# A two-block decoder on one core: layer norms in two parts of two row tiles

## What is computed

```
x = ln(x + causal attention(x))                 # 32 heads, 8 key heads, rope, scaled keys
x = ln(x + fake_quant(x) @ fake_quant(ctx))     # per sequence, 512x512
x = ln(x + stream mixing(x))                    # 24 logits a row, 50 Sinkhorn rounds on 4x4, branch
x = ln(x + gated decay attention(x))            # 32 heads, chunks of 128
x = ln(x + cross attention(x, ctx))             # 32 heads, keys and values of ctx, rms norms
x = ln(x + x @ W.T + bias + low-rank product)   # rank 16 x 3, selected by sequence
```

## Time and profile before

| | us |
|---|---|
| median of 3 runs | 1503.37 |
| lowest and highest | 1503.25, 1508.79 |
| the profiled execution | 1506.34 |
| its span | 1504.5 |
| TensorE busy | 1433.5 (95%) |
| VectorE busy | 1051.2 (70%) |
| ScalarE busy | 808.9 (54%) |
| POOL busy | 582.5 (39%) |

### The profile page before, as it was taken

The page is one execution under the profiler, slowest core; times in us unless marked ns, Lnnn a source line. Parts: engine busy times, 40 slices in busy tenths (PEclk is TensorE's granted clock), DMA queues, the critical chain, the costliest instruction groups (busy, mean ns, idle before and its releaser), DMA issues.

```text
span 1504.5 us, 23551 instructions
## 1 busy us (share of the span) xinstructions
PE 1433.5 (95%) x7346; PEld 1181.5 (79%) x7346; DVE 1051.2 (70%) x2415; ACT 808.9 (54%) x2066; POOL 582.5 (39%) x611
## 2 busy tenths in 40 slices
PE   7999999998999989999999999789999999999976
PEld 5888888886688868778778877578888888888862
DVE  5697666795587876776776687557667676676662
ACT  4556655554223255755765675346656656565440
POOL 4555444433022145655755663323223123132010
PEclk9999999999899999999999999889999999999998
DMA  8011111012023241222133130410201201201000
GB/s 314 1 71 71 71 70 65 10 67 115 0 85 126 85 141 51 104 98 99 56 107 116 33 122 29 182 42 1 84 15 71 85 15 70 76 22 62 1 1 28
DMA packets 30126, 107.66 MB, mean 72 GB/s; under 512 B 3847, under 2 KB 13191, under 8 KB 22104
## 3 DMA queue, kind: packets, MB, share of 16 engines
q1 hardware_dynamic: 30040, 106.58, 19.7%
HBM read 97.07 MB, written 9.50 MB: 71 GB/s over the span
## 4 chain that ended last, share of the span: by engine, by line
PE 64%; issue 13%; DVE 11%; POOL 8%; ACT 3%; DMA 1%; POOLq 0%; SPq 0%; DVEq 0%; ACTq 0%
PE bank L186 11%; PE bank L187 11%; PE bank L188 11%; PE bank L1743 7%; PE bank L1571 6%; PE bank L1729 3%; POOL yss L1377 2%; PE bank L316 2%; PE bank L1687 2%; PE bank L339 1%; POOL wq_low L1018 1%; POOL tmp L159 1%; PE bank L1201 1%; PE bank L285 1%; PE bank L327 1%
## 5 line engine op out<-in xcount | busy, mean ns | idle before, releaser
L159 POOL TENSOR_TENSOR tmp<-tmp,sin 128x512 f32<-128x512 f32 x80 | 111.8, 1397 | 210.9 <-ACT tmp L152 210.9
L2003 DVE SCALAR_TENSOR_TENSOR logit<-bank,qss,amask 128x512 f32<-128x512 f32 x128 | 91.5, 749 | 86.3 <-PE bank L188 85.0
L188 PE MATMUL bank<-wo_low,att_high 128*128 128x512 f32 x384 | 150.7, 393 | 0.0
L1743 PE MATMUL bank<-probT,v 128*128 128x256 f32 x512 | 123.6, 384 | 1.2 <-ACT probT L1849 1.2
L1925 POOL TENSOR_TENSOR qss<-qss,half 128x4 f32<-128x4 f32 x32 | 34.8, 1089 | 229.2 <-DVE qss L1989 229.2
L1849 ACT ACTIVATE probT<-bank 128x512 f32<-128x512 f32 x128 | 69.6, 595 | 86.0 <-PE bank L1729 85.9
L1571 PE MATMUL bank<-kT,wg 128*128 128x256 f32 x512 | 112.9, 383 | 2.9 <-ACT prob L1605 2.9
L1840 ACT ACTIVATE prob<-logit,rmax 128x512 f32<-128x512 f32 x128 | 91.5, 716 | 39.1 <-DVE rmax L2007 39.1
L1571 PEld LDWEIGHTS bank<-kT,wg 128*128 128x128 f32 x512 | 98.1, 192 | 17.2 <-ACT prob L1605 3.3
L186 PE MATMUL bank<-l_wo_high,att_high 128*128 128x512 f32 x256 | 104.9, 410 | 1.8 <-DVE att_low L1461 1.1
L1743 PEld LDWEIGHTS bank<-probT,v 128*128 128x128 f32 x512 | 94.0, 190 | 13.9 <-issue 1.8
(11 more groups left out here) (262 smaller groups left out, 4100.2 us busy)
## 6 DMA issues: line engine op xcount, KB each, us to landing
wq<-in_l_wq SPq DMA_DIRECT2D x16, 1024.0 KB, 5.9
wo<-in_l_wo SPq DMA_DIRECT2D x16, 1024.0 KB, 4.9
wkv<-in_l_wkv SPq DMA_DIRECT2D x16, 512.0 KB, 5.8
wg<-in_l_wg SPq DMA_DIRECT2D x8, 1024.0 KB, 4.8
wq<-in_x_wq SPq DMA_DIRECT2D x8, 1024.0 KB, 7.2
wo<-in_x_wo SPq DMA_DIRECT2D x8, 1024.0 KB, 4.9
kT<-in_x_wkv SPq DMA_DIRECT2D x8, 512.0 KB, 4.2
kv_keys<-logit SPq DMA_DIRECT2D x8, 512.0 KB, 4.7
```

The costliest lines, as they stand in the source:

```text
L159: eng.tensor_tensor(halves(tmp[4 + j % 2]), halves(tmp[2 + j % 2]), per_batch(sin), ALU.mult).then_inc(sem(f"{l}_sinp"), 1)
L188: return eng.matmul(dst, a_high, b_low, start=False, stop=stop)
L1743: last = pe.matmul(bank[VALUE_BANKS[s % 2]][:, 0:L], v[at][:, b * CT + kt, :], probT[s % 2][:, kt, :], start=(kt == 0), stop=(kt == CT - 1))
L2003: dve.scalar_tensor_tensor(logit[s % 2][:, c, :], bank[3 + c][:, :], qss[p][:, 1, h, 2 * b + c:2 * b + c + 1], amask[:, c, :], ALU.mult, A ...
```

## The change

Every norm is cut in two parts, k = 0 with tiles 0 and 1, k = 1 with tiles 2 and 3 (`PAIRS`): `ln_stats`, `ln_spread`, `ln_rows` on VectorE, and `ln_gpsimd`, `ln_tensor`, `ln_scalar`, `ln_split` with an argument k. The power is on two columns. In the three attentions tiles 0 and 1 are added earlier, and their part of the norm stands ahead of the adds of tiles 2 and 3. In the second sublayer the product of tile 0 stands ahead of the first norm's second turns. The second norm's turns stand on both sides of the early unit, and ScalarE squares and copies by parts. In the third norm the rows of tiles 0 and 1 stand ahead of the last statistic. In the last sublayer the low-rank product is done by sequence, in two banks, and the turns of tiles 2 and 3 stand after the four products of tile 0. The selection moves to step 5 of the cross attention's last group, the high query weights to step 5 of the first attention's last group, and POOL's first key power behind both parts of the fourth norm. The fourth norm's tiles are turned into other banks.

```diff
@@ l0_scalar, body
+                    if s == 5 and last:
+                        l1_high_queries(act)
...
                 if last:
                     turned(7)
                     headed(7)
-                    l1_high_queries(act)
@@ l0_vector, body
-                    if s == 7 and not last:
+                    if s == 7:
                         if first:
                             dve.wait_ge(sem("ld_x"), 16)
                         residual_add(dve, "l0", g, 0, bank[0])
...
                 if last:
                     rest(6)
+                    residual_add(dve, "l0", g, 1, bank[1])
+                    ln_stats(dve, 0, 0, "l0_added", 4 * g)
                     rest(7)
-                    homes = [bank[0], bank[1], bank[L0_LATE[0]], bank[L0_LATE[1]]]
-                    sums_and_stats(dve, 0, lambda t: residual_add(dve, "l0", g, t, homes[t]), "l0_added", 4 * g)
+                    ln_rows(dve, 0, 0)
+                    for t in PAIRS[1]:
+                        residual_add(dve, "l0", g, t, bank[L0_LATE[t - 2]])
+                    ln_stats(dve, 0, 1, "l0_added", 4 * g)
@@ the norm's helpers
+        PAIRS = ((0, 1), (2, 3))
+        def turn_bank(n, t):
+            return bank[([0, 1, 2, 5] if n == 3 else [6, 5, 7, 2])[t]]
+        def ln_stats(dve, n, k, done, before):
+            for t in PAIRS[k]:
+                dve.wait_ge(sem(done), before + t + 1)
+                dve.bn_stats(stat[:, t, :], x[:, t, :]).then_inc(sem("ln_stat"), 1)
+            ln_spread(dve, n, k)
+        def ln_spread(dve, n, k):
+            seen = 2 * NT * n + NT * k
+            for i, t in enumerate(PAIRS[k]):
+                dve.wait_ge(sem("ln_stat"), seen + i + 1)
                 dve.bn_aggr(mv[:, t, :], stat[:, t, :]).then_inc(sem("ln_stat"), 1)
+            dve.wait_ge(sem("ln_stat"), seen + NT)
+            dve.tensor_scalar(lnr[:, 0, 2 * k:2 * k + 2], mv[:, 2 * k:2 * k + 2, 1], LN_EPS, None, ALU.add)\
+               .then_inc(sem("ln_var"), 1)
+        def ln_rows(dve, n, k):
+            dve.wait_ge(sem("ln_rstd"), 2 * n + k + 1)
+            for t in PAIRS[k]:
                 dve.tensor_scalar(x[:, t, :], x[:, t, :], mv[:, t, 0:1], lnr[:, 1, t:t + 1],
                                   ALU.subtract, ALU.mult).then_inc(sem("ln_x"), 1)
@@ cross_vector
+            quantised(0)
+            ln_rows(dve, 0, 1)
+            quantised(1)
+            quantised(2)
+            add(0)
+            quantised(3)
+            add(1)
+            ln_stats(dve, 1, 0, "rows_added", 0)
+            ln_rows(dve, 1, 0)
+            add(2)
+            add(3)
+            ln_stats(dve, 1, 1, "rows_added", 0)
+            ln_rows(dve, 1, 1)
@@ mix_scalar
+            for k in range(2):
+                for t in PAIRS[k]:
+                    act.wait_ge(sem("ln_x"), NT * 1 + t + 1)
+                    act.activation(tmp[t][:, :], x[:, t, :], ACT.Square, accum_out=ssq[:, 0, t:t + 1])\
+                       .then_inc(sem("mix_ssq"), 1)
+                ln_scalar(act, 1, k)
+                if k == 0:
+                    kv_copy(act, 1)
@@ mix_vector
                 if t:
                     stats(t - 1)
+                if t == 2:
+                    ln_spread(dve, 2, 0)
+            ln_rows(dve, 2, 0)
             stats(NT - 1)
+            ln_spread(dve, 2, 1)
+            ln_rows(dve, 2, 1)
@@ l1_vector, body
                 gated(3)
+                if last_group:
+                    for t in PAIRS[0]:
+                        residual_add(dve, "l1", g, t, bank[L1_OUT[t]])
                 rest(2)
                 rest(3)
                 if last_group:
+                    ln_stats(dve, 3, 0, "l1_added", 4 * g)
+                    ln_rows(dve, 3, 0)
+                    for t in PAIRS[1]:
+                        residual_add(dve, "l1", g, t, bank[L1_OUT[t]])
+                    ln_stats(dve, 3, 1, "l1_added", 4 * g)
@@ x_vector, body
-                    if s == 7 and not last_group:
+                    if s == 7:
                         add(g, 0)
...
+                    if s == 5 and last_group:
+                        ffn_select(dve)
...
                 if last_group:
                     low(6)
+                    add(g, 1)
+                    ln_stats(dve, 4, 0, "x_added", 4 * g)
                     low(7)
+                    ln_rows(dve, 4, 0)
+                    for t in PAIRS[1]:
+                        residual_add(dve, "x", g, t, bank[t + 1])
+                    ln_stats(dve, 4, 1, "x_added", 4 * g)
+                    ln_rows(dve, 4, 1)
@@ ffn_tensor
             pe.wait_ge(sem("ld_ffn"), 16 * 5)
+            pe.wait_ge(sem("x_added"), 4 * NG)
+            low_rank(0)
+            whole(0)
+            ln_tensor(pe, 4, 1)
+            added(0)
+            whole(1)
+            added(1)
+            low_rank(1)
+            for t in PAIRS[1]:
+                whole(t)
+                added(t)
@@ ffn_vector
+            selected(0)
+            add(0)
+            add(1)
+            selected(1)
+            ln_stats(dve, 5, 0, "rows_added", NT)
+            ln_rows(dve, 5, 0)
+            add(2)
+            add(3)
+            ln_stats(dve, 5, 1, "rows_added", NT)
+            ln_rows(dve, 5, 1)
@@ ScalarE's block
             l0_scalar(act)
+            ln_scalar(act, 0, 0)
             kv_copy(act, 0)
-            ln_scalar(act, 0)
-            kv_copy(act, 1)
+            ln_scalar(act, 0, 1)
             mix_scalar(act)
...
-            x_scalar_first(act)
-            ln_scalar(act, 3, xT_high)
+            for k in range(2):
+                x_squares(act, 0, 0, k)
+                ln_scalar(act, 3, k, xT_high)
@@ POOL's block
             x_gpsimd_first(pool)
-            ln_gpsimd(pool, 3)
+            for k in range(2):
+                ln_gpsimd(pool, 3, k)
+            x_key_pow(pool, 0)
@@ TensorE's block
             l0_tensor(pe)
+            ln_tensor(pe, 0, 0)
             kv_tensor_first(pe, 0)
-            ln_tensor(pe, 0)
-            cross_tensor(pe)
+            cross_tensor(pe, 0)
+            ln_tensor(pe, 0, 1)
+            for t in range(1, NT):
+                cross_tensor(pe, t)
+            ln_tensor(pe, 1, 0)
             kv_tensor_first(pe, 1)
-            ln_tensor(pe, 1)
+            ln_tensor(pe, 1, 1)
             mix_tensor(pe)
             kv_tensor(pe)
+            ln_tensor(pe, 2, 0)
             pe.wait_ge(sem("kv_copied"), 4 * NG)
-            ln_tensor(pe, 2)
+            ln_tensor(pe, 2, 1)
@@ VectorE's block, after l1_vector
             x_vector_first(dve)
-            ln_vector(dve, 3)
-            ln_split(dve, 3)
+            ln_split(dve, 3, 0)
+            ln_rows(dve, 3, 1)
+            ln_split(dve, 3, 1)
             x_vector(dve)
-            ffn_select(dve)
-            ln_vector(dve, 4)
             ffn_vector(dve)
-            ln_vector(dve, 5)
```

More of the change, by code:

```diff
@@ L649, in l0_vector @@
             piped_groups(nc.vector, body)
-        TURN_BANKS = [5, 6, 7, 2]
-        def sums_and_stats(dve, n, add, done, before):
-            for t in range(NT + 1):
-                if t < NT:
-                    add(t)
-                if t:
-                    dve.wait_ge(sem(done), before + t)
-                    dve.bn_stats(stat[:, t - 1, :], x[:, t - 1, :]).then_inc(sem("ln_stat"), 1)
-        def ln_vector(dve, n):
-            for t in range(NT):
-                dve.wait_ge(sem("ln_stat"), 2 * NT * n + t + 1)
-                dve.bn_aggr(mv[:, t, :], stat[:, t, :]).then_inc(sem("ln_stat"), 1)
-            dve.wait_ge(sem("ln_stat"), 2 * NT * (n + 1))
-            dve.tensor_scalar(lnr[:, 0, :], mv[:, :, 1], LN_EPS, None, ALU.add).then_inc(sem("ln_var"), 1)
-            dve.wait_ge(sem("ln_rstd"), n + 1)
-            for t in range(NT):
+        PAIRS = ((0, 1), (2, 3))
@@ L681, in ln_tensor @@
-        def ln_tensor(pe, n):
-            for t in range(NT):
+            pool.tensor_tensor(lnr[:, 1, 2 * k:2 * k + 2], lnr[:, 0, 2 * k:2 * k + 2], half[:, 0:2], ALU.pow)\
+                .then_inc(sem("ln_rstd"), 1)
+        def ln_tensor(pe, n, k):
+            for t in PAIRS[k]:
                 pe.wait_ge(sem("ln_x"), NT * n + t + 1)
                 for c in range(KC):
-                    last = pe.transpose(bank[TURN_BANKS[t]][:, c * P:(c + 1) * P], x[:, t, c * P:(c + 1) * P],
+                    last = pe.transpose(turn_bank(n, t)[:, c * P:(c + 1) * P], x[:, t, c * P:(c + 1) * P],
@@ L686, in ln_tensor, with ln_split @@
                                         ident[:, :])
                 last.then_inc(sem("ln_turn"), 1)
-        def ln_split(dve, n):
-            for t in range(NT):
+        def ln_split(dve, n, k):
+            for t in PAIRS[k]:
                 dve.wait_ge(sem("ln_xT"), NT * n + t + 1)
@@ L720, in cross_vector, with quantised @@
         def cross_vector(dve):
-            q1 = attT[0]
-            for t in range(NT):
+            def quantised(t):
                 dve.wait_ge(sem("ln_xT"), t + 1)
```

(11 more changed lines are left out.)

107 lines of the change are left out of this document (52 added, 55 removed).

## The result

The changed kernel takes 1484.51 us (median of 4 runs, 1483.43 to 1489.12); before takes 1503.31 beside it (4 runs, 1501.69 to 1508.79). The ratio is 0.9874, 95% interval 0.9842 to 0.9907, so 18.8 us faster where 17.7 were forecast and 1485.7 predicted. A second set of 5 runs gave 1486.59 and 0.9868 [0.9849, 0.9887]. The profiled execution took 1483.43 us with a span of 1481.6.

What follows compares the result with a forecast made beforehand. The prediction took TensorE to bound the kernel (64% of the span), with most of the rest around the six layer norms. Gains of 6.8 + 0 + 2.2 + 8.7 = 17.7 us off 1503.4 gave 1485.7 us, range 1480.5 to 1493.5.

Steps and rivals of the forecast that it cites:

- Parts 1 and 2: First norm with the fake-quantised product, second norm with the mixing logits: 6.8 us gained, bounds 5.0 and 8.1.
- Part 3: Third norm: costed at zero, with the load of wg as cover; without that cover a loss of 0.5 us.
- Part 4: Fourth norm, up to the first query product: 2.2 us gained, bounds 0.5 and 3.4.
- Part 5: Fifth norm, low-rank product and sixth norm, with the selection moved: 8.7 us gained, bounds 7.6 and 9.3.
- (a): Lower clock: mixing logits at 1.2 GHz from their start, query products there 2 us longer; 1488.4 us, chance 0.14.
- (c): Slower: the dense stretch of units, 82.90 us from 440.72, runs at 1.2 GHz; 1515.7 us, chance 0.04.
- (b): First norm's power still waits behind POOL's L1018 because ScalarE's high weights come late; 1491.7 us, chance 0.10.
- (d): Swallowed early gain: Sinkhorn window starts the long stretch later, half of parts 1 and 2 lost; 1489.1 us, chance 0.10.

Runs made afterwards that it cites:

- no_part3: The changed kernel with the third norm whole again, its turns all behind the last copy: 1484.14 us, ratio 0.9854 against before.
- no_part5: The changed kernel with fifth and sixth norm and low-rank product whole again, the selection behind the loop: 1498.95 us, ratio 0.9962 against before.
- no_parts12: The changed kernel with first and second norm whole again and the high query weights behind the last head: 1496.5 us, ratio 0.9936 against before.

## Why the prediction was right, and where it was not

**Parts 1 and 2, 6.8: measured 6.6.** The steps held: the power on two columns 0.70 (taken 0.70), L762 from 374.25 (forecast 373.6, and the last out product itself was 0.7 late), two turned tiles in 1.04 (1.05), logits over at 398.0 (398.2, most of them at 2.4 GHz). Two small terms of the sum were wrong and cancel. The power beside quantising, taken at 0.5, cost nothing: POOL took 0.93 instead of 0.70, VectorE's four operations took 0.54, 0.89 and 0.55 as without it. The Trainium skill (SBUF — State Buffer, "Who interferes with whom") has the engine that issues first keep the shared ports for its whole instruction while the other blocks. The trace agrees in part: VectorE's first operation started at 372.10, POOL's power at 372.27, and POOL paid 0.23 us; but VectorE's next operation, from 372.68 on beside a power that ran until 373.20, lost nothing. And the high weights, costed at nothing because ScalarE had 1.8 us of cover, cost 0.45. The cover was right (ScalarE's delay is not on the path for longer than it), but I left out what the moved weights trigger: POOL's low weights now run beside VectorE's normalising of step 6, which took 2.16 us instead of 0.55. There the trace agrees with the rule just named: POOL was at work in four operations of about 1.27 us one after the other, and each of VectorE's two (0.86 and 1.39 us) ended about when one of them did. Of the moved step I had counted ScalarE's and POOL's time, not the neighbour it got.

**Part 3, 0: measured 0.0.** The cover named, the load of wg, ended last in only one of the two profiles of the changed kernel. In the second the chain of waits goes through it, as in the earlier trace rows:

```profile
516.91 6.82 DMA wg<-in_l_wg
523.75 2.19 ACT l_wg_high L1042 x4
```

In the first it doesn't: the chain there goes through VectorE's third norm and 5.30 us of the time-step products (L1076) that took 3.60 in no_part3. wg came 7.3 us sooner, the exponentials behind both (L1094) only 6.7. With that cover gone the part should have cost up to 0.5 by the prediction's own words; undone, it gave nothing back at the same clock, and in the one profile wg then lands later.

**Part 4, 2.2: measured 1.4, uncertain by 1.1.** By the timelines it is 8.45 and 8.12 us from TensorE's last out product to its first query product, as forecast (8, where it was 11). The key mean waited 0.34 us, as named. Not foreseen: POOL's key power, moved behind the norm's power, runs beside the rows of tiles 2 and 3, which took 1.45 us instead of 1.00.

**Part 5, 8.7: measured 8.7.** The low-rank product starts 9.05 us sooner against the last out product (9.0), the last product of all 8.0 (7.8), the tail gained 1.8 instead of 1.4 or 1.1: two rows (0.91), the half power (0.32) and the aggregates (0.06) make 1.3 of it, and from the last row to the end, where SyncE's last stores land, it is 2.7 us instead of 3.2. I had the selection ahead of the normalising of step 5 at 0.5; it stands behind it, delays the next logits by 1.7 us, and 0.2 is left at the last out product. The rows that I built this on ran at 1.2 GHz in part: with TensorE's clock full, the whole form takes 40.6 us from the start of the last out product to the end and the divided one 32.3, so the edit itself is worth 8.3 less the selection.

**What the sum left out goes with the clock**, 3.6 us of the 19.3 between the mean spans. The prediction counted 0.4 us of lower clock as a loss, in part 4. It priced the clock as a risk (rivals (a) and (c)) and not as a gain, though the rows of the fifth norm showed turns at half clock, 3.63 us for 16: removing idle time can remove a fall of the clock. It is shown for the gap of the fifth norm alone, by the two fillings; for the rest of the 3.6 us it is argued. Rival (a) came in halves: the logits ran at 2.4 GHz to their end in the first profile of the changed kernel (3.75 us) and up to their last 1 us in the second (4.10 us), and the clock fell then; the query products had it back 3 us after their start in the first profile, 5 us in the second. Here the transposes matter. The Trainium skill (TensorE: Matmul & The Clock Gate, "Part 4: PE-mode transpose") has them not count as work for the clock; I argued against that from a row in which the clock might have returned for another reason (in no_part5 it stayed at 0.50 through 16 transposes and 4 us of products). The run with 48 transposes disagrees with the page: for keeping the clock up they did what products did, in the one profile of it. Whether transposes bring a fallen clock back it does not show.

**The other rivals.** (b) was prevented by the early weights, and priced right: 6.2 measured, 6 forecast. (c) did not come: the units from 435 to 510 us ran at full clock in every profile. (d) fell with no_parts12.

The total, forecast as 17.7 us and measured as 18.8 between the medians (19.3 between the mean spans), is thus 15.7 at the same clock and 3.6 with it. So the number came out closer than its terms: the edits gave 2.0 less than the sum, the clock 3.6 that the sum did not have, and that the two nearly cancel is luck. The edits undone one by one make 16.7, one more than together, which is the uncertainty of that table.

## What to carry to other kernels

Divide a layer norm where its second half can wait behind other work: count the idle time of the engine that ends last, and the gain is what of it goes, less the extra turns. When a step is moved, price what its follow-up work lands beside, not only the queue it left. And compare kernels at the same mean granted clock before a microsecond is given to an edit: here the runs of one kernel lie up to 8 us apart, and by the fitted slope 6 us of it go with the clock.

## What the runs showed of the hardware

- The clock can be kept up with work that is thrown away: 5.3 us of it in a gap of 6.4 us gave back 3.6 us in all from there to the end; 48 transposes did as well as 22 products (one profile of each). Filling does not always do it: with a gap of 3.7 us filled for 3.0, the clock fell behind it all the same. The same idle time (3.2 us) brought it down in one execution and not in another.
- POOL and VectorE slow each other at times: two VectorE operations of 128 columns took 2.16 us beside POOL's four fp32r subtractions of 512 columns (0.55 alone), two of 512 columns 1.45 beside a POOL power of 8 columns (1.00 alone), and four quantising operations nothing beside one of 2 columns, which itself took 0.93 us instead of 0.70.
- A POOL power on 128 rows takes 0.70 us for 2 columns, 1.01 for 4 and 1.63 for 8.
